# First loads from ScalarE's queue, LoRA lots held behind them, a new order of set one's copies, and inputs laid out by partition

## The chip, the core and the metric

The kernel runs on one core of a Trainium2 chip. The metric is the device time of one execution in microseconds (us), lower is better. The core has a matrix engine (TensorE, PE in the profile, with PEld for its weight loads), VectorE (DVE), ScalarE (ACT), GpSimd (POOL) and SyncE (SP), which here does nothing but issue transfers. Transfers are issued by SP or by ACT. Engines are in order: an instruction that waits holds all that stand behind it on its engine.

## The reference, cut to what matters

```python
# x [2, 1024, 256]; ids [2], the LoRA expert of each sequence; F = 1024, E = 8, TOP_K = 2
h = x @ wi.T + 2 * (x @ common_a.T) @ common_b.T + 2 * (x @ own_a[ids].T) @ own_b[ids].T
h = relu(h)
c = h @ wo.T + (the same two LoRA terms for the way down)
probs = softmax(mean(c, over tokens) @ gate_w)          # one router decision per sequence
top_w, top_i = top_k(probs, 2); top_w /= sum(top_w)
out = x + sum over the two experts e of top_w * (gelu(c @ w1[e] + b1[e]) @ w2[e] + b2[e])
```

All is f32 in and out.

## The kernel before

**Precision.** Every product of two f32 tensors is made of three products of "high" and "low" parts. The high part is a copy to the fp32r type (on ScalarE, functions named `..._high`), the low part is the f32 original less the high part (on VectorE or GpSimd, `..._low`). A product is high x high, high x low and low x high, each a 128 x 128 by 128 x 512 matmul (`three`).

**Work.** Tokens are two sequences (b = 0, 1) of 1,024, each in two halves t of 512. The 1,024 hidden units are cut into four sets of 256. A set q (24 in all: 8 of the conditional part, then 16 of the experts) has an up weight tile `up_raw` and a down weight tile `down_raw` of 256 KB each, a ring of three buffers for each. The hidden layer of a set is four tiles j (two blocks f of hidden units by two token halves t), each in one bank of `hid_ps`; the down products add into the four banks of `out_ps`. Sets 0 to 7 use plain products, sets 8 to 23 a seven-product scheme.

**LoRA.** In the conditional part the LoRA terms are merged into the weights first: TensorE multiplies the two small factors (`raw_up_factor`, `up_factor`, `down_factor`), VectorE adds twice the result to the raw weights (`merge0`, `merge_up`, `merge_down`), and only then come the high and low copies. Set 0 and set 1 take their up factors raw from `lora_first` and `lora_second`; all others need the split factors in `lora_st`, which come from five lots of 192 KB a sequence, (b, 0) to (b, 4), each with a high copy on ScalarE (`lora_high`) and two low halves (`lora_low`). The down weights of set 0 need lot (0, 1), the up weights of set 2 need (0, 0) and (0, 3), the down weights of set 1 need (0, 1) and (0, 2).

**The beginning.** TensorE does twelve warm-up products, the raw factors (L823), then `first_pair(0)` and `first_pair(1)`: set 0's hidden tiles for token half 0 and then half 1, in the order high x high (L743), the low of x (L747), the low of the weights (L751), 12 products each. Then come the down factor of set 0 (L845), tiles 0 and 1 of set 1 (12 products on lines 700, 701 and 704), `down(0, 0)`, the up factor of set 2 (L835), `down(0, 1)`, the down factor of set 1 (L845), and so on in a repeating order. The order on each engine is written out by hand; semaphores tie them together. x arrives in four transfers: half 0 of sequence 0 as two pieces (below called x0[0] and x0[1], by kd, the half of the model dimension, 256 KB each), half 1 of it in one (x0b, 512 KB), and sequence 1 (1 MB). Before the change, ScalarE's queue issues x0[0] and the up weights of set 0; all the rest goes out from SyncE, in the order lora_first, lora_second, x0[1], up weights of set 1, x0b, then the lots and weights in turn. ScalarE's first instructions are these two issues, then its table load, then the copies.

**Waits that matter below.** `hid_high(1, 0)` overwrites the hidden tile that `down(0, 0)` reads, so it waits for it; `lora_high(0, 2)` stands behind it. `bank_free` makes tile j of set q wait for `hid_low(q - 1, j)`. The up factor of set 2 uses bank 3 and waits for `hid_low(0, 3)`.

Of the kernel before, what the change touches and what calls it, by code (L numbers as in the profile page):

```python
# [19 lines left out]
def build(nc, ids, xT, wiT, woT, lora, gate, w1, w2, b12, outT):  # L20
    D, NTOK = xT.shape
    F = wiT.shape[1]
# [90 lines left out]
    LORA_LO_AT = {0: [(0, 3), (0, 2)], 1: [(0, 4)], 2: [(1, 0)], 3: [(1, 1), (1, 2)], 4: [(1, 3), (1, 4)]}  # L113
# [6 lines left out]
    with ExitStack() as ctx:  # L120
# [9 lines left out]
        x_sb = sb("x_sb", [P, KD, NTOK])  # L130
# [66 lines left out]
        s_x0lo = [sem(f"s_x0lo{kd}") for kd in range(KD)]  # L197
# [78 lines left out]
        def raw_tile(p, kd, t):  # L276
            return x_sb[:, kd, half(1, t)] if p == 0 else y_sb[:, kd, t * TOK:(t + 1) * TOK]
# [6 lines left out]
        def store_final(eng, n):  # L284
# [4 lines left out]
                          x_sb[:, kd, at + cols.start:at + cols.stop]).then_inc(s_out, 16)  # L289
# [4 lines left out]
        def _(eng):  # L294
# [37 lines left out]
            eng.dma_start(x_sb[:, :, SEQ:2 * SEQ], xT[:, SEQ:2 * SEQ].rearrange("(k p) t -> p k t", p=P))\  # L332
# [19 lines left out]
            for b in range(NB):  # L352
                for k in range(TOP_K):
# [4 lines left out]
                    for i in range(SETS):  # L358
                        q = N_COND + (TOP_K * b + k) * SETS + i
                        eng.wait_ge(*up_lo_made(q - NU))  # L360
                        src = w1[bass.ds(e_bk, 1), :, i * SW:(i + 1) * SW].rearrange("e (k p) f -> p (e k) f", p=P)
                        eng.dma_start(up_raw[:, q % NU, 0:4 * P].rearrange("p (k f) -> p k f", k=KD), src)\
                           .then_inc(s_up_raw[q % NU], 16)
                        eng.wait_ge(s_down_lo, q - ND + 1)
                        src = w2[bass.ds(e_bk, 1), i * SW:(i + 1) * SW, :].rearrange("e (f p) d -> p (e f) d", p=P)
                        eng.dma_start(down_raw[:, q % ND, :].rearrange("p (f d) -> p f d", d=D), src)\
                           .then_inc(s_down_raw[q % ND], 16)

            for n, (kd, t) in enumerate(ENDS):
# [822 lines left out]
```

## Time and profile before

| what | value |
|---|---|
| median of 3 runs | 274.09 us (273.92 to 274.73) |
| the profiled execution's own time | 273.91 us |
| its span, first to last instruction | 272.1 us |
| TensorE busy | 263.6 us, 97% |
| ScalarE busy | 170.8 us, 63% |
| VectorE busy | 162.2 us, 60% |
| GpSimd busy | 149.1 us, 55% |
| moved by transfers | 19.10 MB, 70 GB/s over the span |

Times inside the execution are us from its first instruction. The profiled execution took 273.91 us in all, 1.8 more than its span, and it is 0.18 under the median.

### The profile page before, as it was taken

The numbers are of one execution on the slowest core, as the hardware profiler recorded it, in microseconds if no ns is written. First come the engines' busy times: TensorE is split into PE (matmuls) and PEld (weight loads), VectorE is DVE, ScalarE is ACT, GpSimd is POOL, SyncE is SP. The second block draws the span as 40 slices with busy tenths as digits, with TensorE's granted clock in tenths as the row PEclk, the third lists the DMA queues.
The fourth block names the chain that finished last, engine by engine and source line by source line (L and its number), as shares of the span: only waits on it lengthen the run. The fifth ranks groups of instructions, "written<-read, shape, count | busy, mean of one in ns | idle before, by whom it ended". The sixth has DMA issues, their size and how long they took to land.

```text
span 272.1 us, 3590 instructions
## 1 busy us (share of the span) xinstructions
PE 263.6 (97%) x1156; PEld 213.0 (78%) x1156; DVE 162.2 (60%) x266; ACT 170.8 (63%) x275; POOL 149.1 (55%) x181
## 2 busy tenths in 40 slices
PE   7798999999999999999999999999999999999995
PEld 3466888888888888888888788888788888888883
DVE  1664354342469754667486786666965667665664
ACT  2554543535446448997986977776766776775650
POOL 0466343726565677799709999566365465431100
PEclk9999999999999999999999999999999999999999
DMA  5996302201003221122010322023022025000004
GB/s 148 259 319 203 110 7 70 78 2 40 1 2 118 77 77 41 39 77 78 28 51 0 79 77 79 8 69 78 5 76 78 4 76 184 9 0 4 0 0 154
DMA packets 17266, 19.10 MB, mean 70 GB/s; under 512 B 2016, under 2 KB 14592, under 8 KB 17248
## 3 DMA queue, kind: packets, MB, share of 16 engines
q1 hardware_dynamic: 16544, 17.96, 21.9%
q10 hardware_dynamic: 704, 0.92, 1.1%
q8 instruction: 9, 0.15, 0.2%
q14 instruction: 9, 0.07, 0.1%
HBM read 16.77 MB, written 2.10 MB: 69 GB/s over the span
## 4 chain that ended last, share of the span: by engine, by line
PE 93%; DMA 2%; DVE 1%; ACT 1%; SPq 1%; issue 1%; POOL 0%; DVEq 0%; POOLq 0%
PE out_ps L700 16%; PE out_ps L701 16%; PE out_ps L704 16%; PE hid_ps L700 14%; PE hid_ps L701 14%; PE hid_ps L704 14%; DMA x_sb<-in_xT 2%; PE hid_ps L845 1%; PE hid_ps L835 1%; SPq L296 1%; PE hid_ps L747 1%; DVE act_lo L261 0%; DVE up_raw L950 0%; ACT up_hi L535 0%; PE hid_ps L751 0%
## 5 line engine op out<-in xcount | busy, mean ns | idle before, releaser
L700 PE MATMUL out_ps<-hid_hi,down_hi 128*128 128x512 f32 x192 | 75.0, 391 | 0.3 <-issue 0.3
L403 POOL TENSOR_TENSOR up_lo<-up_raw,up_hi 128x512 fp32r<-128x512 f32 x39 | 50.4, 1311 | 45.4 <-ACT up_hi L535 45.3
L701 PE MATMUL out_ps<-hid_lo,down_hi 128*128 128x512 f32 x192 | 74.7, 389 | 0.0
L704 PE MATMUL out_ps<-hid_hi,down_lo 128*128 128x512 f32 x192 | 74.7, 389 | 0.0
L700 PE MATMUL hid_ps<-act_hi,up_hi 128*128 128x512 f32 x168 | 65.7, 391 | 0.0
L701 PE MATMUL hid_ps<-act_lo,up_hi 128*128 128x512 f32 x168 | 65.5, 390 | 0.0
L704 PE MATMUL hid_ps<-act_hi,up_lo 128*128 128x512 f32 x168 | 65.4, 389 | 0.0
L567 ACT ACTIVATE hid_ps<-hid_ps,bias_sb 128x512 f32<-128x512 f32 x64 | 42.2, 659 | 29.7 <-DVE hid_ps L990 19.0
L966 DVE SCALAR_TENSOR_TENSOR hid_lo<-hid_ps,mix,hid_hi 128x512 fp32r<-128x512 f32 x64 | 47.8, 747 | 18.7 <-ACT hid_hi L581 18.2
L409 POOL TENSOR_TENSOR down_lo<-down_raw,down_hi 128x512 fp32r<-128x512 f32 x24 | 31.7, 1321 | 44.0 <-ACT down_hi L545 43.9
L581 ACT ACTIVATE hid_hi<-hid_ps,mix 128x512 fp32r<-128x512 f32 x64 | 44.1, 688 | 4.6
L700 PEld LDWEIGHTS out_ps<-hid_hi,down_hi 128*128 128x128 f32 x192 | 36.0, 188 | 8.6 <-issue 1.1
L704 PEld LDWEIGHTS out_ps<-hid_hi,down_lo 128*128 128x128 f32 x192 | 36.0, 188 | 7.6
L701 PEld LDWEIGHTS out_ps<-hid_lo,down_hi 128*128 128x128 f32 x192 | 36.1, 188 | 7.3
L575 ACT ACTIVATE hid_hi<-hid_ps 128x512 fp32r<-128x512 f32 x32 | 18.9, 595 | 30.9 <-PE out_ps L704 29.3
L990 DVE TENSOR_TENSOR hid_ps<-hid_ps,r_sb 128x512 f32<-128x512 f32 x48 | 31.9, 694 | 8.5 <-PE hid_ps L704 8.5
L700 PEld LDWEIGHTS hid_ps<-act_hi,up_hi 128*128 128x128 f32 x168 | 31.6, 188 | 6.7 <-ACT r_sb L552 0.4
L704 PEld LDWEIGHTS hid_ps<-act_hi,up_lo 128*128 128x128 f32 x168 | 31.5, 188 | 6.7
L701 PEld LDWEIGHTS hid_ps<-act_lo,up_hi 128*128 128x128 f32 x168 | 31.6, 188 | 5.9
L966 DVE SCALAR_TENSOR_TENSOR hid_lo<-hid_ps,hid_hi 128x512 fp32r<-128x512 f32 x32 | 21.8, 683 | 22.1 <-ACT hid_hi L575 22.0
L535 ACT ACTIVATE up_hi<-up_raw 128x1024 fp32r<-128x1024 f32 (+1 forms) x23 | 21.3, 925 | 10.0 <-DVE up_raw L950 5.7
L981 DVE TENSOR_TENSOR r_sb<-hid_ps,r_sb 128x512 f32<-128x512 f32 x16 | 11.0, 690 | 16.1 <-PE hid_ps L704 16.0
(91 smaller groups left out, 217.2 us busy)
## 6 DMA issues: line engine op xcount, KB each, us to landing
up_raw<-in_w SPq DMA_DIRECT2D x16, 256.0 KB, 3.0
down_raw<-in_w SPq DMA_DIRECT2D x16, 256.0 KB, 2.7
down_raw<-in_woT SPq DMA_DIRECT2D x8, 256.0 KB, 3.1
lora_raw<-in_lora SPq DMA_DIRECT2D x10, 192.0 KB, 4.6
up_raw<-in_wiT SPq DMA_DIRECT2D x7, 256.0 KB, 3.7
outT<-x_sb SPq DMA_DIRECT2D x6, 256.0 KB, 3.2
x_sb<-in_xT SPq DMA_DIRECT2D x1, 1024.0 KB, 10.5
x_sb<-in_xT SPq DMA_DIRECT2D x1, 512.0 KB, 6.3
```

The lines of the kernel that those rows point to most:

```text
L403: ins = eng.tensor_tensor(up_lo[:, n, cols], up_raw[:, n, cols], f32(up_hi[:, n, cols]), ALU.subtract)
L409: eng.tensor_tensor(down_lo[:, n, :], down_raw[:, n, :], f32(down_hi[:, n, :]), ALU.subtract)\
L535: eng.activation(up_hi[:, n, 0:up_width(q)], up_raw[:, n, 0:up_width(q)], ACT.Copy).then_inc(s_up_hi, 1)
L567: eng.activation(hid_ps[:, j, :], hid_ps[:, j, :], ACT.Gelu, bias=bias_sb[:, b, k, f:f + 1])\
L575: eng.activation(hid_hi[:, j, :], hid_ps[:, j, :], ACT.Relu).then_inc(s_hid_hi, 1)
L581: eng.activation(hid_hi[:, j, :], hid_ps[:, j, :], ACT.Copy, scale=mix[:, b, k:k + 1])\
L700: eng.matmul(out, w_h, a_h, start=start, stop=False, skip_group_check=onto)
L701: eng.matmul(out, w_h, a_l, start=False, stop=False, skip_group_check=onto)
L704: return eng.matmul(out, w_l, a_h, start=False, stop=stop, skip_group_check=onto)
L966: eng.scalar_tensor_tensor(out=hid_lo[:, j, :], in0=hid_ps[:, j, :], scalar=scalar, in1=f32(hid_hi[:, j, :]), op0=op, op1=ALU.subtract).th ...
L981: eng.tensor_tensor(r3_sb[:, :], hid_ps[:, 2, :], r2_sb[:, :], ALU.add).then_inc(s_r3, 1)
L990: eng.tensor_tensor(hid_ps[:, j, :], hid_ps[:, bank, :], addend[:, :], ALU.add).then_inc(s_add, 1)
```

## The change

Five things are done together.

1. ScalarE's queue now issues five transfers before its first copy: x0[0], the up weights of set 0, x0[1], x0b, the up weights of set 1. SyncE issues lora_first and lora_second, and then waits until x0[1] has landed before it issues the lots and all that stands behind them. Lot (0, 0) goes ahead of the down weights of set 0.
2. Low parts of x: GpSimd now makes x0[0]'s, VectorE the other three. x's low parts have a semaphore for each piece.
3. VectorE now makes the low parts of lots (0, 1), (0, 0) and (0, 3), GpSimd only (0, 2) in this stretch; `merge_down(0)` moves ahead of `hid_low(0, 1)`.
4. ScalarE copies x0b ahead of the up weights of set 1, `hid_high(0, 0)` ahead of them too, lot (0, 1) before `hid_high(0, 1)`, and lot (0, 3) right behind the down weights of set 0.
5. The down products wait for the high part of the down weights first, and for the low part only at the third product of a set. All inputs but the LoRA lots and the small tables are laid out on the host so that each partition's part of a transfer is one piece (2 KB of weights or of x0[0], 4 KB of x0b, 8 KB of sequence 1), and `x_sb` has the same layout.

```diff
-    LORA_LO_AT = {0: [(0, 3), (0, 2)], 1: [(0, 4)], 2: [(1, 0)], 3: [(1, 1), (1, 2)], 4: [(1, 3), (1, 4)]}
+    LORA_LO_AT = {0: [(0, 2)], 1: [(0, 4)], 2: [(1, 0)], 3: [(1, 1), (1, 2)], 4: [(1, 3), (1, 4)]}
...
-        x_sb = sb("x_sb", [P, KD, NTOK])
+        x_sb = sb("x_sb", [P, NB, NT, KD, TOK])
...
-        s_x0lo = [sem(f"s_x0lo{kd}") for kd in range(KD)]
+        s_x0lo = [[sem(f"s_x0lo{kd}{t}") for t in range(NT)] for kd in range(KD)]
...
         def load_up(eng, q):
             n, i = q % NU, q % SETS
-            eng.dma_start(up_raw[:, n, 0:4 * P].rearrange("p (k f) -> p k f", k=KD),
-                          wiT[:, i * SW:(i + 1) * SW].rearrange("(k p) f -> p k f", p=P)).then_inc(s_up_raw[n], 16)
+            eng.dma_start(up_raw[:, n, 0:4 * P], wiT[i, :, :]).then_inc(s_up_raw[n], 16)
 
         def load_down(eng, q):
             n, i = q % ND, q % SETS
-            eng.dma_start(down_raw[:, n, :].rearrange("p (f d) -> p f d", d=D),
-                          woT[i * SW:(i + 1) * SW, :].rearrange("(f p) d -> p f d", p=P)).then_inc(s_down_raw[n], 16)
+            eng.dma_start(down_raw[:, n, :], woT[i, :, :]).then_inc(s_down_raw[n], 16)
 
         def load_x0(eng, kd):
-            eng.dma_start(x_sb[:, kd, half(0, 0)], xT[kd * P:(kd + 1) * P, half(0, 0)]).then_inc(s_x0[kd], 16)
+            eng.dma_start(x_sb[:, 0, 0, kd, :], xT[0, :, 0, kd, :]).then_inc(s_x0[kd], 16)
 
         def up_lo_made(q):
             return (s_up0lo, KD) if q == 0 else (s_up_lo, q)
 
         def x0_low(eng, kd, t):
             eng.wait_ge(s_x0hi, t * KD + kd + 1)
-            eng.tensor_tensor(act_lo[:, 0, kd * NT + t, :], x_sb[:, kd, half(0, t)],
-                              f32(act_hi[:, 0, kd * NT + t, :]), ALU.subtract).then_inc(s_x0lo[kd], 1)
+            eng.tensor_tensor(act_lo[:, 0, kd * NT + t, :], x_sb[:, 0, t, kd, :],
+                              f32(act_hi[:, 0, kd * NT + t, :]), ALU.subtract).then_inc(s_x0lo[kd][t], 1)
...
-            load_x0(eng, 1)
-            next_up(1)
-            eng.dma_start(x_sb[:, :, half(0, 1)], xT[:, half(0, 1)].rearrange("(k p) t -> p k t", p=P))\
-               .then_inc(s_x0b, 16)
+
+            eng.wait_ge(s_x0[1], 16)
             load_lora(0, 1, e)
+            load_lora(0, 0, e)
             next_down(0)
-            load_lora(0, 0, e)
             load_lora(0, 3, e)
             next_up(2)
             load_lora(0, 2, e)
             next_down(1)
             load_lora(0, 4, e)
-            eng.dma_start(x_sb[:, :, SEQ:2 * SEQ], xT[:, SEQ:2 * SEQ].rearrange("(k p) t -> p k t", p=P))\
+            eng.dma_start(x_sb[:, 1, :, :, :], xT[1, :, :, :, :])\
                .then_inc(s_x1, 16)
             next_down(2)
             next_up(3)
...
-            x0_low(eng, 1, 0)
+            x0_low(eng, 0, 0)
             up_low(1)
-            x0_low(eng, 1, 1)
-            after((s_x0lo[1], NT))
-            lora_low(0, 1)
             down_low(0)
             after((s_down_lo, 1))
             lora_lows(0)
...
             load_x0(eng, 0)
             load_up(eng, 0)
+            load_x0(eng, 1)
+            eng.dma_start(x_sb[:, 0, 1, :, :], xT[0, :, 1, :, :]).then_inc(s_x0b, 16)
+            load_up(eng, 1)
             x0_high(0)
             x0_high(1)
             up0_high(0)
             up0_high(1)
-            up_high(1)
             x0b_high(0)
             x0b_high(1)
             hid_high(0, 0)
+            up_high(1)
+            lora_high(0, 1)
             hid_high(0, 1)
-            lora_high(0, 1)
             lora_high(0, 0)
             hid_high(0, 2)
             down_high(0)
+            lora_high(0, 3)
             for q in range(1, NSET):
...
-                if q == 1:
-                    lora_high(0, 3)
...
-            def down_pair(q, j, kd):
+            def down_pair(q, j, kd, low_ready=None):
...
-                    eng.wait_ge(s_down_lo, q + 1)
+                    eng.wait_ge(s_down_hi, q + 1)
                 if q in GROUP_FIRST:
                     out_free(q, j)
                 for kd in range(KD):
-                    ins = down_pair(q, j, kd)
+                    ins = down_pair(q, j, kd, (s_down_lo, q + 1) if j + kd == 0 else None)
                 ins.then_inc(s_down, 1)
...
-            x0_low(eng, 0, 0)
             merge0(0)
             merge0(1)
+            x0_low(eng, 1, 0)
             up0_low(0)
             up0_low(1)
+            x0_low(eng, 0, 1)
             merge_up(1, out_ps[:, 2, :])
-            x0_low(eng, 0, 1)
+            x0_low(eng, 1, 1)
+            lora_low(0, 1)
             hid_low(0, 0)
+            merge_down(0, out_ps[:, 3, :])
             hid_low(0, 1)
-            merge_down(0, out_ps[:, 3, :])
+            lora_low(0, 0)
             hid_low(0, 2)
-            lora_low(0, 0)
+            lora_low(0, 3)
             for q in range(1, N_COND):
...
+    def up_sets(w):
+
+        w = w.reshape(w.shape[:-2] + (D // P, P, F // SW, SW))
+        return np.moveaxis(w, -2, -4).swapaxes(-3, -2).reshape(w.shape[:-4] + (F // SW, P, D // P * SW))
+
+    def down_sets(w):
+
+        w = w.reshape(w.shape[:-2] + (F // SW, SW // P, P, D))
+        return w.swapaxes(-3, -2).reshape(w.shape[:-4] + (F // SW, P, SW // P * D))
...
-        "xT": t(x.reshape(NB * S, D)),
-        "wiT": t(a["L0_cond_wi"]),
-        "woT": t(a["L0_cond_wo"]),
+        "xT": x.reshape(NB, S // TOK, TOK, D // P, P).transpose(0, 4, 1, 3, 2),
+        "wiT": up_sets(t(a["L0_cond_wi"])),
+        "woT": down_sets(t(a["L0_cond_wo"])),
         "lora": np.concatenate(lots, axis=2),
         "gate": a["L0_ffn_gate_w"],
-        "w1": a["L0_ffn_w1"],
-        "w2": a["L0_ffn_w2"],
-
+        "w1": up_sets(a["L0_ffn_w1"]),
+        "w2": down_sets(a["L0_ffn_w2"]),
```

## Rows read from the trace of the kernel before

**Rows 1.** busy by stretch: length, each engine (instructions), PE clock, DMA share, GB/s

```profile
0.00:9.08 9.08, 6.33 (x21) 2.89 (x21) 2.08 (x6) 3.00 (x5) 0.91 (x13) 1.00 0.62 169
...
24.77:268.90 244.13, 244.08 (x1084) 201.18 (x1084) 149.47 (x246) 159.49 (x255) 138.46 (x159) 1.00 0.17 52
268.90:272.10 3.20, 0.00 (x0) 0.00 (x0) 0.88 (x2) 0.00 (x0) 0.00 (x0) 1.00 0.46 164
```

**Rows 2.** timeline of PE: start us, us long, line; idle before, releaser

```profile
5.96 1.12 PE L823 MATMUL out_ps<-lora_first 32*128 32x256 f32 x4 [0.43 <-DMA lora_first<-in_lora]
...
9.08 0.70 PE L743 MATMUL hid_ps<-act_hi,up_hi 128*128 128x512 f32 x2 [1.12 <-ACT up_hi L525]
...
12.44 0.73 PE L743 MATMUL hid_ps<-act_hi,up_hi 128*128 128x512 f32 x2 [0.39 <-ACT act_hi L513]
13.82 0.73 PE L747 MATMUL hid_ps<-act_lo,up_hi 128*128 128x512 f32 x2 [0.65 <-DVE act_lo L261]
...
16.59 0.50 PE L845 MATMUL out_ps<-lora_st 96*128 96x256 f32 x2
...
20.18 0.47 PE L700 MATMUL out_ps<-hid_hi,down_hi 128*128 128x512 f32 x1 [0.35 <-issue]
...
21.92 0.47 PE L835 MATMUL hid_ps<-lora_st 96*128 96x256 f32 x2
...
24.77 0.47 PE L845 MATMUL hid_ps<-lora_st 96*128 96x256 f32 x2 [1.01 <-POOL lora_st L232]
```

**Rows 3.** timeline of ACT, up to 31 us

```profile
1.64 1.28 ACT L509 ACT_TABLE_LOAD   x1 [1.64 <-PEq L1182]
...
8.00 0.63 ACT L509 ACTIVATE act_hi<-x_sb 128x512 fp32r<-128x512 f32 x1 [2.70 <-DMA x_sb<-in_xT]
8.53 0.71 ACT L525 ACTIVATE up_hi<-up_raw 128x256 fp32r<-128x256 f32 x2
...
22.34 0.62 ACT L519 ACTIVATE lora_st<-lora_raw 96x512 fp32r<-96x512 f32 x1
```

**Rows 4.** timeline of SP, the issues of three transfers

```profile
3.61 0.42 SPq L254 DMA_DIRECT2D x_sb<-in_xT  x1
...
4.55 0.47 SPq L322 DMA_DIRECT2D x_sb<-in_xT  x1
5.21 0.34 SPq L302 DMA_DIRECT2D lora_raw<-in_lora  x1
```

**Rows 5.** transfers issued to 30 us: KB each, median us to landing

```profile
lora_raw<-in_lora SPq DMA_DIRECT2D x9, 192.0 KB, 6.5
...
x_sb<-in_xT SPq DMA_DIRECT2D x1, 512.0 KB, 6.3
x_sb<-in_xT ACTq DMA_DIRECT2D x1, 256.0 KB, 3.9
up_raw<-in_wiT ACTq DMA_DIRECT2D x1, 256.0 KB, 4.3
x_sb<-in_xT SPq DMA_DIRECT2D x1, 256.0 KB, 4.4
```

**Rows 6.** timeline of DVE, the first merge of up weights

```profile
6.78 0.77 DVE L937 SCALAR_TENSOR_TENSOR up_raw<-out_ps,up_raw 128x256 f32<-128x256 f32 x2 [0.76 <-PE out_ps L823]
```

**Rows 7.** line 261, low parts of x: ns shortest, median, longest

```profile
L261 DVE TENSOR_TENSOR act_lo<-x_sb,act_hi x2: 691/1020/1348, 5.3 to 12.4; 128x512 fp32r<-128x512 f32 x2
L261 POOL TENSOR_TENSOR act_lo<-x_sb,act_hi x2: 1281/1512/1742, 8.7 to 13.2; 128x512 fp32r<-128x512 f32 x2
```

**Rows 8.** line 232, low parts of lots, up to 30 us

```profile
L232 DVE TENSOR_TENSOR lora_st<-lora_raw,lora_st x2: 415/904/1394, 18.5 to 19.0; 32x256 fp32r<-32x256 f32 x2
```

**Rows 9.** timeline of POOL, low parts of lot (0, 2)

```profile
23.10 1.53 POOL L232 TENSOR_TENSOR lora_st<-lora_raw,lora_st 32x256 fp32r<-32x256 f32 x2 [1.33 <-ACT lora_st L519]
```

**Rows 10.** transfers from 4 to 5 us by queue (q10 ACT's, q1 SP's)

```profile
q1 hardware_dynamic: 104, 0.13, 46.8%
q10 hardware_dynamic: 114, 0.10, 33.4%
```

More of the change, by code:

```diff
@@ L20, in build @@
 def build(nc, ids, xT, wiT, woT, lora, gate, w1, w2, b12, outT):
-    D, NTOK = xT.shape
-    F = wiT.shape[1]
+    D, NTOK = outT.shape
+    F = wiT.shape[0] * 2 * P
     E = w1.shape[0]
@@ L276, in raw_tile @@
         def raw_tile(p, kd, t):
-            return x_sb[:, kd, half(1, t)] if p == 0 else y_sb[:, kd, t * TOK:(t + 1) * TOK]
+            return x_sb[:, 1, t, kd, :] if p == 0 else y_sb[:, kd, t * TOK:(t + 1) * TOK]
         ENDS = [(0, 0), (1, 0), (0, 1), (1, 1)]
@@ L288, in store_final @@
             eng.dma_start(outT[kd * P:(kd + 1) * P, at + cols.start:at + cols.stop],
-                          x_sb[:, kd, at + cols.start:at + cols.stop]).then_inc(s_out, 16)
+                          x_sb[:, NB - 1, t, kd, cols]).then_inc(s_out, 16)
         program = ctx.enter_context(nc.Block())
@@ L360, in _ @@
                         eng.wait_ge(*up_lo_made(q - NU))
-                        src = w1[bass.ds(e_bk, 1), :, i * SW:(i + 1) * SW].rearrange("e (k p) f -> p (e k) f", p=P)
-                        eng.dma_start(up_raw[:, q % NU, 0:4 * P].rearrange("p (k f) -> p k f", k=KD), src)\
-                           .then_inc(s_up_raw[q % NU], 16)
+                        src = w1[bass.ds(e_bk, 1), i, :, :].rearrange("e p c -> (e p) c")
+                        eng.dma_start(up_raw[:, q % NU, 0:4 * P], src).then_inc(s_up_raw[q % NU], 16)
                         eng.wait_ge(s_down_lo, q - ND + 1)
-                        src = w2[bass.ds(e_bk, 1), i * SW:(i + 1) * SW, :].rearrange("e (f p) d -> p (e f) d", p=P)
-                        eng.dma_start(down_raw[:, q % ND, :].rearrange("p (f d) -> p f d", d=D), src)\
-                           .then_inc(s_down_raw[q % ND], 16)
+                        src = w2[bass.ds(e_bk, 1), i, :, :].rearrange("e p c -> (e p) c")
+                        eng.dma_start(down_raw[:, q % ND, :], src).then_inc(s_down_raw[q % ND], 16)
             for n, (kd, t) in enumerate(ENDS):
                 eng.wait_ge(s_fin, n + 1)
-                eng.dma_start(outT[kd * P:(kd + 1) * P, half(0, t)], x_sb[:, kd, half(0, t)]).then_inc(s_out, 16)
+                eng.dma_start(outT[kd * P:(kd + 1) * P, half(0, t)], x_sb[:, 0, t, kd, :]).then_inc(s_out, 16)
             for n in (0, 2, 4):
@@ L508, in x0_high @@
                 eng.wait_ge(s_x0[kd], 16)
-                eng.activation(act_hi[:, 0, kd * NT, :], x_sb[:, kd, half(0, 0)], ACT.Copy).then_inc(s_x0hi, 1)
+                eng.activation(act_hi[:, 0, kd * NT, :], x_sb[:, 0, 0, kd, :], ACT.Copy).then_inc(s_x0hi, 1)
             def x0b_high(kd):
                 eng.wait_ge(s_x0b, 16)
-                eng.activation(act_hi[:, 0, kd * NT + 1, :], x_sb[:, kd, half(0, 1)], ACT.Copy).then_inc(s_x0hi, 1)
+                eng.activation(act_hi[:, 0, kd * NT + 1, :], x_sb[:, 0, 1, kd, :], ACT.Copy).then_inc(s_x0hi, 1)
             def lora_high(b, lot):
@@ L598, in raw_high @@
                     eng.wait_ge(s_x1, 16)
-                    src = x_sb[:, kd, SEQ:2 * SEQ]
+                    src = x_sb[:, 1, :, kd, :]
                 else:
@@ L775, in down_pair @@
                              (hid_hi[:, j, :], hid_lo[:, j, :]), q in GROUP_FIRST and j == mine[0],
-                             q in GROUP_LAST and j == mine[1])
+                             q in GROUP_LAST and j == mine[1], low_ready)
             def out_free(q, j):
@@ L996, in result @@
                 for kd in range(KD):
-                    eng.scalar_tensor_tensor(out=x_sb[:, kd, half(b, t)], in0=out_ps[:, kd * NT + t, :],
-                                             scalar=mixed_b2[:, b, 1, kd:kd + 1], in1=x_sb[:, kd, half(b, t)],
+                    eng.scalar_tensor_tensor(out=x_sb[:, b, t, kd, :], in0=out_ps[:, kd * NT + t, :],
+                                             scalar=mixed_b2[:, b, 1, kd:kd + 1], in1=x_sb[:, b, t, kd, :],
                                              op0=ALU.add, op1=ALU.add).then_inc(s_fin, 1)
@@ L1135, in _ @@
             for n, (kd, t, cols) in enumerate(FINAL):
-                at = half(NB - 1, t).start
-                mine = slice(at + cols.start, at + cols.stop)
+                x = x_sb[:, NB - 1, t, kd, cols]
                 eng.wait_ge(s_done, ENDS.index((kd, t)) + 1)
-                eng.scalar_tensor_tensor(out=x_sb[:, kd, mine], in0=out_ps[:, kd * NT + t, cols],
-                                         scalar=mixed_b2[:, NB - 1, 1, kd:kd + 1], in1=x_sb[:, kd, mine],
+                eng.scalar_tensor_tensor(out=x, in0=out_ps[:, kd * NT + t, cols],
+                                         scalar=mixed_b2[:, NB - 1, 1, kd:kd + 1], in1=x,
                                          op0=ALU.add, op1=ALU.add).then_inc(s_final, 1)
```

7 lines of the change are left out of this document (3 added, 4 removed).

## The prediction, made before the change was run

> **What bounds the kernel now.** I read the busy time by stretch first, then what TensorE waited for, then the timelines of the first 31 us. The table has its answer in one row: from 24.77 to 268.90 us TensorE is busy for 244.08 of 244.13 us [rows 1], 1,084 products at 0.225 us apiece, at the full granted clock of 1.00 (its 2.4 GHz level). After 24.77 nothing that arrives earlier can help, and the tail behind the last product (3.20 us) holds the same instructions in both kernels. So whatever the change is worth, it is worth by moving the down factor of set 1, which starts at 24.77 [rows 2], and every other engine's work behind it hangs on semaphores that move with it.
>
> From its first real product at 9.08 to 24.77 TensorE has 48 products of 512 columns (10.8 us at 0.225) and two factor steps of 0.34 and 0.31, 11.45 in all [rows 2]. 24.77 less 9.08 is 15.69, so 4.24 us are waits: pair 0 to pair 1 takes 3.36 for 2.7 of work (the 12.44 row, x0b late); 12.44 to 13.82 takes 1.38 for two products, 0.45 (VectorE's low part of x), and the rest of pair 1, to 16.59, holds another 0.5; the start of `down(0, 0)` at 20.18 comes 3.59 after the down factor at 16.59, for 0.34 and 2.7 of work; the up factor at 21.92 comes 1.74 after it for 1.35; and 24.77 comes 2.85 after that, for 0.31 and 1.35 [rows 2]. That is 0.66, 0.93, 0.5, 0.55, 0.4 and 1.2. Ahead of 9.08 TensorE waits on ScalarE: x0[1] lands at 8.0 (3.61 and 4.4), is copied from 8.00, and only then come the copies of set 0's merged up weights at 8.53 [rows 3, 4, 5].
>
> **The change part by part.** Landings are a transfer's issue plus its time to landing [rows 4, 5]: now x0[1] 8.0, x0b 10.85, lot (0, 1) 11.7 (with the median of nine).
>
> *Start.* x0[1] is issued third by ScalarE, at 1.65 instead of 3.61 (issues cost 0.42 to 0.47 [rows 4]). If all the 1.96 us counted it would land at 6.0; if the engines and not the issue are what it waits for, still at 8.0. I take 6.6, nearer the early end, because lora_first no longer stands ahead of it in its queue. Its copy ends at 7.2. Now the merge is as late: raw factors need lora_first, first product 5.96, merge from 6.78, two halves in 0.77, so the first is done at 7.2 and the second at 7.55 [rows 2, 6]. The copy of the first half of set 0 takes 0.40 (two in 0.71 [rows 3]), and TensorE follows 0.15 after it, as 8.53 and 0.40 led to 9.08. So the first product goes from 9.08 to 7.75: **1.33 less**. With x0[1] later than 6.6 the start moves one for one. Three more issues on ScalarE (1.3 us) push its table load from 1.64 to 2.95 and its end to 4.25; x0[0] lands at 4.64 (0.74 and 3.9 [rows 5]), so this is hidden by 0.4 us.
>
> *Low parts of x.* GpSimd makes x0[0]'s (1.28 us [rows 7]) at 5.4 to 6.7, needed at 8.2. VectorE makes x0[1]'s from 7.5 to 8.2 (0.69 uncontended [rows 7]), needed at 9.1, then set 0's low weights until 9.0, needed at 9.55. VectorE and GpSimd block each other when both read only SBUF: 0.69 became 1.35, and for a half lot 0.415 became 1.39 [rows 7, 8]. Here they no longer meet in this stretch. Pair 0 is then 2.7 without a wait: 7.75 to 10.45.
>
> *x0b and set 1's up weights.* x0b is issued at 2.1 instead of 4.55 and no longer behind the 256 KB of up weights. Ends: 8.4 (2.45 earlier) and 10.85. I take 8.7. Its copies end at 9.35 and 9.9, needed at 10.45 and 11.35. Up weights of set 1 now stand behind it: I take 9.5 (from 8.6, 4.08 and the 4.5 or so of the others, to 10.85). VectorE then does x0b's first low part 9.4 to 10.1, `merge_up(1)` to 10.7, the second low part to 11.35, needed at 11.8. Pair 1 has no wait either: 10.45 to 13.15.
>
> *The wait on SyncE.* Behind it stand all lots, the down weights of sets 0 to 2, up weights of sets 2 and 3, and x of sequence 1. The first issue there moves from 5.21 to 6.65, but with 1 MB less ahead in its queue. Ends for lot (0, 1): 9.55, with three quarters of the 3.9 that 256 KB took on an empty queue, and 13.1, with the 6.5 of now [rows 5]. I take 10.5, nearer the empty queue that it finds, and 0.8 more for each next one. ScalarE wants (0, 1) at 11.35, (0, 0) at 12.4, (0, 3) at 15.3; VectorE the down weights at 14.1. Hidden by 0.9 us and more; past that it costs one for one. Sets 2 on are wanted at 19 and later.
>
> *Lots on VectorE.* ScalarE copies lot (0, 1) at 11.35 to 11.95. VectorE's two halves then meet GpSimd's low part of set 1's up weights (11.5 to 12.8); blocked as in [rows 8] they end at 13.45 instead of 12.8. The down factor of set 0 starts at 13.45 against 16.59: 0.3 of wait is new. `hid_low(0, 0)` stands behind them and ends at 14.1, and set 1's first tile waits for it; 0.3 again. Its 12 products end at 16.85. `merge_down(0)` from 14.1 to 14.8, `down_high(0)` to 15.45, GpSimd's low part to 16.9. `down(0, 0)` now starts on the high part at 16.85 and wants the low part at 17.3: the 0.55 of wait is gone. **20.18 becomes 16.85, 3.33 less.**
>
> *What is late next.* Two things feed 24.77. From `down(0, 0)`: its end frees the tile, ScalarE copies it and then lot (0, 2) (22.34), GpSimd makes the low parts in 1.53 from 23.10, TensorE follows [rows 2, 3, 9]. None of this is changed, so the distance 20.18 to 24.77, 4.59, stays: 16.85 and 4.59 is 21.45. The other: VectorE has `lora_low(0, 0)` against GpSimd's 1.3 us (ends 17.3, blocked again), `hid_low(0, 2)` to 17.95, `lora_low(0, 3)` to 18.75, `hid_low(0, 3)` to 19.4, and the up factor of set 2 waits for that; 19.4, 0.31 and 1.35 is 21.1. It is hidden by 0.35. So 24.77 becomes 21.45.
>
> *Layout.* Half as many rows for each weight transfer. With 1 KB rows 256 KB took 4.3 from ScalarE's queue and with 2 KB rows 3.9 [rows 5], so a load gains between 0 and 0.4; I take 0, since the loads up to 21 us are hidden above and those behind it feed a TensorE that never waits [rows 1]. The copy of sequence 1 from two pieces instead of one: nothing, for the same reason.
>
> **Sum.** 1.33 (start), 0.66, 0.93, 0.5 and 0.55 (waits that go), less 0.6 (two new ones): 3.4, and by the rounded steps above 3.3, which 24.77 moves by, since what lies between `down(0, 0)` and it keeps its length. Against its own time: 273.91 less 3.3 is 270.6. The median is 0.18 above that execution, so 270.7.
>
> **A page against the estimate.** The Trainium skill, page "DMA: Bandwidth & Descriptors", section "Issuing engines are not separate DMA queues", says that a second issuing engine saves only the sequencer's issue time. By that rule x0[1] can gain at most the 1.96 us, which the sum respects, and bytes that had landed by a certain time land no sooner; this is the late-loads rival below, at the time that is worked out there from rows.
>
> **Rivals.** *x0[1] as late as before* (it is the read and not the issue). The start stays at 9.08, the later waits still go: 3.3 less 1.3, 271.9. For it: x0[0], alone in its queue, took 3.9 too [rows 5].
>
> *Late loads.* x0b and set 1's up weights need, with all that is ahead, the same 1,632 KB that had landed at 10.85. If the up weights land then, `merge_up(1)` ends at 12.0, the low part of x0b behind it at 12.65 (0.35 of wait), ScalarE's copy, GpSimd's low part and the blocked lot slip by 1.2, and the down factor starts at 14.65: 3.3 less 1.2, 271.9. The lot at its late end, 13.1, gives the same: copied to 13.7, its low parts to 14.6 (GpSimd is done by then). Against it: from 4 to 5 us the engines were 0.80 busy (46.8% and 33.4% [rows 10]), so there is room.
>
> *The queues are drained in the order of issue, as one* (the slower side). Then lora_first, issued at 2.64, stands behind all five of ScalarE's transfers, and the start is its landing plus 1.8. It decides from a landing of 9.2 us on (now 5.9, and 3.3 of gain); with the 1,632 KB landed at 10.85 the start is at 12.65 and the sum 4.9 less 3.3 on the wrong side: 275.5. Against it: from 4 to 5 us packets of both queues were served side by side [rows 10], though ScalarE's were issued 1.5 us ahead.
>
> *The gain is given back*: the first 25 us shrink, and a wait opens behind 24.77, for instance on a load held back on SyncE. 273.9. For it only that such waits do not show until something moves; against it that the only clocks there are semaphores of TensorE's own progress.
>
> **Chances.** Forecast 0.66, x0[1] late 0.12, late loads 0.12, drained as one 0.04, given back 0.06. The likeliest has 270.1 to 271.3 of its own (landings of x0[1] 0.5 either way, one more or one fewer blocking). The range reaches to the two at 271.9 and half a us beyond, and down to 269.9, where lora_first too lands 0.7 sooner: 269.9 to 272.4. A measurement here can tell 0.3%, 0.8 us, from no change; faster by more holds the first three, 0.90; the same 0.06; slower 0.04.
>
> **What would show it.** x0[1]'s copy starting near 6.6 and TensorE's first L743 near 7.75; no wait at the second L743 and the second L747; L845 of set 0 near 13.45, released by VectorE; `down(0, 0)` near 16.85; L845 of set 1 near 21.45, released by GpSimd's lot (0, 2); from there on 244.1 us of uninterrupted products. Wrong if lora_first lands later than 6.5, if the low part behind `merge_up(1)` ends after 11.8, if `hid_low(0, 3)` ends after 19.7, or if the stretch behind set 1's down factor is longer than 244.13.

## The result: 0.4% slower, where 1.2% faster was forecast

| | before | changed |
|---|---|---|
| median, 22 executions each | 274.1 us (273.56 to 274.92) | 275.63 us (274.42 to 276.68) |
| ratio, with its 95% interval | | 1.0044 (1.0029 to 1.0059) |
| the profiled execution | 273.91 us, span 272.1 | 274.78 us, span 273.0 |

The forecast was 270.7 with a range up to 272.4. The direction was wrong.

The busy time by stretch of the changed kernel: up to pair 0, pair 0 itself, and from the down factor of set 1 on. The columns are those of [rows 1]: length, busy time of PE, PEld, DVE, ACT and POOL, granted clock, DMA share, GB/s.

```profile
0.00:10.00 10.00, 7.46 (x21) 2.97 (x21) 2.10 (x6) 3.68 (x6) 1.80 (x13) 1.00 0.75 235
10.00:14.44 4.44, 4.44 (x14) 3.50 (x14) 2.25 (x5) 0.94 (x3) 0.00 (x0) 0.62 1.08 280
...
25.59:269.70 244.11, 244.02 (x1084) 201.18 (x1084) 149.56 (x247) 160.11 (x256) 138.57 (x159) 1.00 0.16 52
269.70:273.00 3.30, 0.00 (x0) 0.00 (x0) 0.85 (x2) 0.00 (x0) 0.00 (x0) 1.00 0.46 161
```

The last two rows are as forecast: 244.11 us in which TensorE is busy for 244.02, against 244.13 and 244.08 in [rows 1], and a tail of 3.3 against 3.2. Nothing was gained or lost behind the down factor of set 1. That factor starts at 25.59 instead of 24.77 [rows 2] or the forecast 21.45; the whole result is in front of it. The second row has one of the two reasons: a mean granted clock of 0.62 in pair 0, where the same stretch of the kernel before has 1.00:

```profile
9.08:12.44 3.36, 2.97 (x13) 2.14 (x13) 2.14 (x4) 1.36 (x4) 1.40 (x2) 1.00 1.03 281
```

The other is the length of the first row. The timeline of TensorE in the changed kernel, with the columns of [rows 2] (the first row is the warm-up products):

```profile
1.20 5.30 PE L872 MATMUL hid_ps<-y_sb 128*128 128x512 bf16 x12 [1.20 <-DVE y_sb L1059]
7.59 1.13 PE L817 MATMUL out_ps<-lora_first 32*128 32x256 f32 x4 [1.09 <-DMA lora_first<-in_lora]
8.97 1.10 PE L817 MATMUL out_ps<-lora_second,lora_first 32*128 32x256 f32 x4 [0.25 <-DMA lora_second<-in_lora]
10.00 0.78 PE L737 MATMUL hid_ps<-act_hi,up_hi 128*128 128x512 f32 x2
...
14.44 0.62 PE L737 MATMUL hid_ps<-act_hi,up_hi 128*128 128x512 f32 x2
...
17.44 0.50 PE L839 MATMUL out_ps<-lora_st 96*128 96x256 f32 x2
18.25 0.47 PE L694 MATMUL hid_ps<-act_hi,up_hi 128*128 128x512 f32 x1 [0.31 <-DVE hid_lo L960]
...
21.07 0.39 PE L694 MATMUL out_ps<-hid_hi,down_hi 128*128 128x512 f32 x1
...
23.60 0.50 PE L829 MATMUL hid_ps<-lora_st 96*128 96x256 f32 x2 [1.01 <-DVE hid_lo L960]
...
25.59 0.48 PE L839 MATMUL hid_ps<-lora_st 96*128 96x256 f32 x2
```

The raw factors wait 1.09 us for lora_first, the second four for lora_second, and the first real product starts at 10.00, not at 7.75 as forecast or 9.08 as before. Then pair 0 takes 4.44 us for 2.7 us of work. From 14.44 on each piece has the length that was forecast within a quarter of a us: 3.00, 3.63 and 4.52 us where the prediction had 3.0, 3.4 and 4.6, with the forecast waits on VectorE in front of 18.25 (0.31) and 23.60 (1.01). Where lora_first was is in the view of transfers issued up to 30 us (columns of [rows 5]):

```profile
x_sb<-in_xT ACTq DMA_DIRECT2D x2, 256.0 KB, 3.8
...
x_sb<-in_xT ACTq DMA_DIRECT2D x1, 512.0 KB, 5.2
lora_first<-in_lora SPq DMA_DIRECT2D x1, 64.0 KB, 4.9
lora_second<-in_lora SPq DMA_DIRECT2D x1, 32.0 KB, 5.6
```

The up weights of set 1 alone, ScalarE's last load, in the same view cut to the time of their issue:

```profile
up_raw<-in_wiT ACTq DMA_DIRECT2D x1, 256.0 KB, 6.0
```

And ScalarE's timeline, with the last two of its five issues:

```profile
2.12 0.45 ACTq L626 DMA_DIRECT2D x_sb<-in_xT  x1
2.60 0.45 ACTq L247 DMA_DIRECT2D up_raw<-in_wiT  x1
3.09 1.28 ACT L502 ACT_TABLE_LOAD   x1 [3.09 <-issue]
4.42 0.63 ACT L502 ACTIVATE act_hi<-x_sb 128x512 fp32r<-128x512 f32 x1
5.69 0.63 ACT L502 ACTIVATE act_hi<-x_sb 128x512 fp32r<-128x512 f32 x1 [0.64 <-DMA x_sb<-in_xT]
```

SyncE issued lora_first at 2.63, 0.03 us behind ScalarE's last load, and it landed 4.9 us later, at 7.55; in the kernel before it had been issued at the same time and its first product ran at 5.96 [rows 2]. Between 4 and 5.5 us, well after both issues, only ScalarE's queue moves anything:

```profile
DMA packets 259, 0.59 MB, mean 391 GB/s; under 512 B 30, under 2 KB 30, under 8 KB 259
...
q10 hardware_dynamic: 259, 0.59, 104.3%
```

In the kernel before, both queues moved packets from 4 to 5 us [rows 10]. From 6 to 7.5 us both queues move packets in the changed kernel too:

```profile
q10 hardware_dynamic: 179, 0.35, 68.8%
q1 hardware_dynamic: 105, 0.13, 34.8%
```

So lora_first landed behind the first four of ScalarE's loads (the fourth, x0b, at 7.3), but not behind the fifth: the up weights of set 1, issued 0.03 us ahead of it, landed at 8.6, 1.1 us after it.

What arrived early did so by more than forecast: x0[0] was copied at 4.42 and x0[1] at 5.69, where 6.6 was taken for the latter and 6.0 had been the early end, and x0b landed at 7.3 (2.12 and 5.2), where 8.7 was taken. It bought nothing, since the copy of set 0's up weights needs the merge and the merge needs lora_first.

### The profile page after: what moved, and what is told of

Same layout as the page of the kernel before. It is cut to its first block, busy times and chain, and to the rows that moved or that the text cites. A ratio compares the mean times of both kernels' runs of the same rounds, so it can differ in the third digit from the quotient of the medians.

```text
span 273.0 us, 3575 instructions
## 1 busy us (share of the span) xinstructions
PE 265.6 (97%) x1156; PEld 214.6 (79%) x1156; DVE 163.5 (60%) x271; ACT 171.1 (63%) x275; POOL 144.6 (53%) x176
## 4 chain that ended last, share of the span: by engine, by line
PE 92%; DVE 3%; DMA 2%; SPq 1%; ACT 1%; issue 0%; DVEq 0%
PE out_ps L694 16%; PE out_ps L698 16%; PE out_ps L695 16%; PE hid_ps L694 14%; PE hid_ps L695 14%; PE hid_ps L698 14%; DMA lora_second<-in_lora 2%; DVE lora_st L234 2%; DVE hid_lo L960 1%; PE hid_ps L839 1%; PE hid_ps L829 1%; PE hid_ps L741 1%; SPq L296 1%; PE hid_ps L737 1%; PE out_ps L817 0%
```

## The experiments

The three parts of the change are called the layout, the queues (ScalarE's five loads and SyncE's wait) and the order (of copies and low parts). All ratios are to the kernel before on the same chip. A "fall" is a stretch at the low clock. One like that in the second row above takes the mean clock of the execution from 1.00 to 0.993 or 0.994 (the changed kernel's profile has 0.994); 0.987 or 0.988 is about twice that time at the low clock. The diffs are against the changed kernel unless another is named.

**e1: lora_first ahead of x0b and set 1's up weights.**

```diff
 # ScalarE
             load_x0(eng, 1)
-            eng.dma_start(x_sb[:, 0, 1, :, :], xT[0, :, 1, :, :]).then_inc(s_x0b, 16)
-            load_up(eng, 1)
 # SyncE, behind lora_second
+            eng.dma_start(x_sb[:, 0, 1, :, :], xT[0, :, 1, :, :]).then_inc(s_x0b, 16)
+            next_up(1)
             eng.wait_ge(s_x0[1], 16)
```

> The changed kernel, with x0b and set 1's up weights issued by SyncE behind lora_second instead of by ScalarE ahead of it; ScalarE keeps x0[0], the up weights of set 0 and x0[1]. Theory A (transfers are served in the order of issue whatever the queue, so lora_first landed at 7.55 behind 1,280 KB): lora_first lands near 6.0, behind 768 KB, the raw factors start there instead of at 7.59, the first L737 near 7.9 instead of 10.00, and if the granted clock then stays at 1.00 the time is 2.5 to 4 us under the changed kernel's 274.6, near 271. Theory B (the loss is VectorE's new order in set one): lora_first may land earlier, but the down factor of set 1 stays near 25.5 and the time within 0.8 us of the changed kernel's. Theory C (lora_first is late because SyncE's own queue starts late): lora_first still lands after 7 us.

Measured: 271.85 us, ratio 0.9915 (0.9903 to 0.9928). (In the changed kernel 1,536 KB are issued ahead of lora_first; the 1,280 KB of the expectation are what landed ahead of it.) The landing of lora_first and TensorE's timeline:

```profile
lora_first<-in_lora SPq DMA_DIRECT2D x1, 64.0 KB, 3.6
```

```profile
6.29 1.12 PE L816 MATMUL out_ps<-lora_first 32*128 32x256 f32 x4 [0.50 <-DMA lora_first<-in_lora]
...
8.33 1.22 PE L736 MATMUL hid_ps<-act_hi,up_hi 128*128 128x512 f32 x2
...
12.79 0.62 PE L736 MATMUL hid_ps<-act_hi,up_hi 128*128 128x512 f32 x2
...
23.93 0.47 PE L838 MATMUL hid_ps<-lora_st 96*128 96x256 f32 x2
```

Issued at 2.64, lora_first lands at 6.25, and the first product starts 1.67 us earlier than in the changed kernel. Of theory A the early landing and the time hold, though the start is at 8.33 and not near 7.9; B and C fall: the order on VectorE is the same and 23.93 is 1.66 ahead of 25.59. This profiled execution still has the slow clock in pair 0 (8.33 to 12.79 is 4.46 us), and it is the longest of the six: 273.13 at a mean clock of 0.993, the other five 271.16 to 271.95 at 0.998 to 1.000. So one fall of the clock costs some 1.3 us here. Of the 3.5 us by which e1 is under the changed kernel by the ratios, the earlier start is worth some 1.5 (273.13 against the changed kernel's 274.58, the median of its executions with one fall); the rest is that the clock falls in one of six executions and not in all. In all runs the loads in front of lora_first were ScalarE's; whether large loads of SyncE's own queue would hold up a small one of ScalarE's was not tried.

**e2: four more warm-up products.** The edit is `WARM_UP = 16`.

> The changed kernel with 16 warm-up products instead of 12, nothing else. They fill the gap from 6.50 to 7.59 in which TensorE has nothing to do. Theory A with the clock as a second loss (pair 0 ran at a granted clock of 0.50 from 10.53 to 13.95 because TensorE had idled before it): the clock stays at 1.00, pair 0 takes 2.7 instead of 4.4 us, and the time is 1.3 to 1.7 us under the changed kernel's. Theory D (the clock is a lottery of the execution and the gap has no part in it): no difference to the changed kernel within 0.5 us, and the clock still falls in the profiled execution.

Measured: 273.11 us, ratio 0.9981 (0.9963 to 0.9999), so some 1.7 to 2.5 under the changed kernel by the medians. TensorE's timeline:

```profile
1.20 5.39 PE L872 MATMUL hid_ps<-y_sb 128*128 128x512 bf16 x16 [1.20 <-DVE y_sb L1059]
7.49 1.13 PE L817 MATMUL out_ps<-lora_first 32*128 32x256 f32 x4 [0.91 <-DMA lora_first<-in_lora]
...
9.94 0.73 PE L737 MATMUL hid_ps<-act_hi,up_hi 128*128 128x512 f32 x2
...
12.79 0.62 PE L737 MATMUL hid_ps<-act_hi,up_hi 128*128 128x512 f32 x2
...
23.96 0.47 PE L839 MATMUL hid_ps<-lora_st 96*128 96x256 f32 x2
```

lora_first is as late as ever (7.49), the start is at 9.94, but pair 0 is over at 12.79, 2.85 us. Nine of the twelve executions have a mean clock of 0.998 or more and take 272.87 to 273.28; the three at 0.993 and 0.994 take 274.30 to 275.21. The changed kernel has no execution over 0.994 among 33 (22, and 11 more in e12): 17 have one fall, 0.993 or 0.994, and a median of 274.58; 16 have 0.981 to 0.988, twice as long at the low clock or longer, and a median of 276.18. Theory D falls: four more products make the falls rare. That they do it by filling the gap is not shown. In this profile the sixteen products took 5.39 us, hardly longer than the twelve of the changed kernel (5.30), 0.91 us of gap were left in front of lora_first against 1.09, and the clock did not fall.

**e3: the layout alone.** The kernel before with loads and `x_sb` by partition; all issues, copies and low parts in the old order.

> The kernel before with the new layout alone (inputs by partition, x_sb too): loads issued from the old queues in the old order, old order of copies and low parts. Theory A: landings come 0.5 to 1.5 us earlier in the first 20 us, because packets of 2 KB and more are served faster; the start moves with x0[1] alone, so 0 to 1.5 us under the kernel before. Rival: no difference (0.3 us), since TensorE waits for other engines and not for bytes.

Measured: 274.04 us, ratio 1.0000 (0.9990 to 1.0011). The rival holds. x0[1] still came for a start at 9.16:

```profile
9.16 1.19 PE L739 MATMUL hid_ps<-act_hi,up_hi 128*128 128x512 f32 x2 [1.21 <-ACT up_hi L522]
...
13.41 0.61 PE L739 MATMUL hid_ps<-act_hi,up_hi 128*128 128x512 f32 x2
...
16.69 0.50 PE L841 MATMUL out_ps<-lora_st 96*128 96x256 f32 x2
...
24.88 0.47 PE L841 MATMUL hid_ps<-lora_st 96*128 96x256 f32 x2 [0.98 <-POOL lora_st L234]
```

This profile says one thing more. The clock fell here too, pair 0 takes 4.25 us (9.16 to 13.41) instead of 3.36, and yet the down factor of set 0 is at 16.69 and that of set 1 at 24.88, 0.1 behind [rows 2]. The kernel before waits for x0b behind pair 0 anyway, and the slow products fit into that wait. It shows in the times of the kernel before that were taken beside e1 to e12: 24 at a clock of 0.998 to 1.000 have a median of 273.95, 32 at 0.992 to 0.994 one of 274.00; only the six with 0.987 or 0.988 are longer, 274.79. One fall of the clock is free in the old kernel and costs 1.3 us (e1) to 1.9 (e9) in one that no longer waits.

**e4: layout and new order, old queues.**

> The changed kernel with its loads issued as before the change (x0[1], set 1's up weights and x0b by SyncE behind lora_second, no wait on SyncE, old order of down weights and lot (0, 0)); new layout and new order of copies and low parts stay. Theory A: lora_first lands near 5.9, the start is as in the layout alone, and the new order saves the waits in pair 1 and before down(0, 0): 2 to 3 us under the kernel before. Theory B (the new order is what costs): slower than the layout alone by 0.8 us or more.

Measured: 273.84 us, ratio 0.9981 (0.9964 to 0.9999). Neither: 2 to 3 us were expected and 0.2 to 0.5 came. With the old queues x0[1] lands as late as before; the start is at 9.53. Only two of twelve executions were free of a fall, and these took 272.39 and 272.44, 1.6 under before; in the other ten the waits of the old order are replaced by a slow pair 0 (4.33 us in the profile). The new order saves 1.6 us where the clock stays up (e3's three executions without a fall have a median of 274.05) and 0.2 where it falls. This is a miss of A in the median, and what A left out was the clock.

**e5: layout and queues, old order.**

> The changed kernel with the old order of copies and low parts; the new layout, ScalarE's five loads and SyncE's wait stay. Theory A (order of issue): lora_first lands near 7.5 as in the changed kernel, so the first product of set 0 starts near 10.0; x0b is there early but the old order copies it only behind set 1's up weights, so waits in pair 1 stay: 0.5 to 1.5 us over the kernel before, 274.6 to 275.5. Theory B (the new order of low parts is what costs): under the kernel before, since x0b and set 1's weights land 2 us earlier.

Measured: 275.82 us, ratio 1.0079 (1.0049 to 1.0110). The raw factors start at 7.87, the first product at 10.20. The time is 0.3 over theory A's range. The queues alone do the damage, and the new order does not add to it; theory B falls.

**e6: e1 with 16 warm-up products.** `WARM_UP = 16` on e1.

> e1 (x0b and set 1's up weights issued by SyncE behind lora_second) with 16 warm-up products. The two losses should be separate: the earlier lora_first gave 2.8 us at the median, and the clock still fell in e1's profiled execution (273.13 against its median of 271.85). Theory A with the clock: the time is e1's best, 271.2 to 271.8, the high single times of e1 go, the clock stays at 1.00 in the profile. Rival: warm-up products do nothing once lora_first is early; median 271.85 and one in six executions near 273 as in e1.

Measured: 272.10 us, ratio 0.9935 (0.9922 to 0.9948). The expectation is missed: no clock under 0.998 in five executions, but the median is not better than e1's. e7's profile suggests why.

**e7: the two chains behind `down(0, 0)`.** On e6:

```diff
-    LORA_LO_AT = {0: [(0, 2)],
+    LORA_LO_AT = {0: [(0, 3), (0, 2)],
 # ScalarE, set 1
+                if q == 1:
+                    lora_high(0, 2)
                 if cond(q):
                     hid_high(q, 0)
-                    if q == 1:
-                        lora_high(0, 2)
 # VectorE, set 0
             hid_low(0, 2)
-            lora_low(0, 3)
```

> e6 with two edits to what feeds set 2's up factor and set 1's down factor: GpSimd makes lot (0, 3)'s low parts again (VectorE's hid_low(0, 3) moves up by 0.86), and ScalarE copies lot (0, 2) ahead of hid_high(1, 0), not behind it. Theory (both chains named in the prediction bind, each by about 1 us): the wait before L828 of 1.0 and the one before L838 of 0.3 go down by 0.9 in all, and the time is 0.7 to 1.2 us under e6. Rival: GpSimd's queue (low parts of the down weights, then two lots) becomes the late one, and the time is e6's within 0.3 us.

Measured: 271.43 us, ratio 0.9896 (0.9883 to 0.9910), 1.1 us under e6 by the ratios. The wait of 1.01 before the up factor of set 2 is 0.15, and the down factor of set 1 comes 1.71 behind it, not 1.98. Three rows of this profile bear on e6:

```profile
1.20 6.57 PE L871 MATMUL hid_ps<-y_sb 128*128 128x512 bf16 x16 [1.20 <-DVE y_sb L1058]
7.69 1.13 PE L816 MATMUL out_ps<-lora_first 32*128 32x256 f32 x4
...
9.61 0.72 PE L736 MATMUL hid_ps<-act_hi,up_hi 128*128 128x512 f32 x2
```

lora_first had landed at 6.35, but the sixteen warm-up products took 6.57 us here, until 7.77 (5.16 in e6's profile, which is e6's fastest execution), so the raw factors started at 7.69 and the first product at 9.61. Warm-up products that outlast the load they cover delay what stands behind them. That the slower executions of e6 are such ones is likely and not shown.

**e8: only x0b behind lora_second.** Set 1's up weights stay on ScalarE's queue.

> The changed kernel with only x0b moved behind lora_second on SyncE's queue; set 1's up weights stay on ScalarE's. A dose between e1 and the changed kernel: bytes issued ahead of lora_first are 1,024 KB, against 768 KB in e1 (landed 6.25) and 1,536 KB less the last, issued in the same 0.03 us, in the changed kernel (landed 7.55). Theory A (order of issue): lora_first lands at 6.6 to 7.0 and the first L737 starts between e1's 8.33 and the changed kernel's 10.00, near 8.8 to 9.1. Rival (only x0b with its 4 KB packets holds lora_first up): it lands at 6.25 as in e1.

Measured: 275.77 us, ratio 1.0049 (1.0032 to 1.0067). The landing:

```profile
lora_first<-in_lora SPq DMA_DIRECT2D x1, 64.0 KB, 5.0
```

That is 7.65, later than expected (6.6 to 7.0) and no better than in the changed kernel, with a third less ahead of it; the size of the dose was missed. What holds is the order: the up weights of set 1, issued 0.5 us ahead of it, land at 7.2, then lora_first, lora_second and x0b follow in the order of their issue. The rival, that only x0b is in the way, falls. What is left open is why 512 KB less ahead of it brought lora_first no earlier (7.65 against 7.55): the bytes ahead do not give the landing.

**e9: e7 with 12 warm-up products.**

> e7 with 12 warm-up products instead of 16 (so: the changed kernel, x0b and set 1's up weights on SyncE behind lora_second, lot (0, 3)'s low parts on GpSimd, lot (0, 2) copied ahead of hid_high(1, 0)). In e7's profile the 16 products ran at the low clock until 7.77 and held the raw factors back from 6.35 to 7.69. Theory: 12 products lose nothing on that side, so the median is 0 to 0.5 us under e7's ratio of 0.9896, and 0.7 to 1.2 us under e1. Rival: without the four products the clock falls more often and the median is over e7's.

Measured: **270.36 us, ratio 0.9879 (0.9855 to 0.9902)**, the best version. TensorE's timeline:

```profile
1.19 5.29 PE L871 MATMUL hid_ps<-y_sb 128*128 128x512 bf16 x12 [1.19 <-DVE y_sb L1058]
6.42 1.13 PE L816 MATMUL out_ps<-lora_first 32*128 32x256 f32 x4
...
8.34 0.73 PE L736 MATMUL hid_ps<-act_hi,up_hi 128*128 128x512 f32 x2
...
19.55 0.47 PE L828 MATMUL hid_ps<-lora_st 96*128 96x256 f32 x2 [0.19 <-POOL lora_st L234]
...
21.25 0.40 PE L838 MATMUL hid_ps<-lora_st 96*128 96x256 f32 x2
```

Five of six executions have a clock of 1.000 and take 269.91 to 270.63; the sixth has a fall and takes 272.15. By the ratios e9 is 1.0 us under e1, as expected, and 0.5 under e7, where the two intervals overlap. The down factor of set 1 is at 21.25, which is where the prediction had put it (21.45), by another way: 0.6 later at the start, and 0.8 less behind it. The 0.6 at the start is the warm-up again: lora_first landed at 5.9, and the twelve products ran until 6.48.

**e10: e1's queues, old order.**

> e1's queues (three loads on ScalarE, x0b and set 1's up weights behind lora_second on SyncE, wait on SyncE) with the old order of copies and low parts. It fills the table of load order by copy order. Theory: the new order pays only where the data is early, so here it should show: e10 is 1.5 to 2.5 us over e1 (ratio near 0.998 to 1.000 of before). Rival: the queues alone make e1's gain and the order is worth nothing, e10 within 0.4 us of e1.

Measured: 273.92 us, ratio 0.9993 (0.9976 to 1.0011), 2.1 us over e1. The theory holds. What TensorE waited for, us in total, times, longest:

```profile
PE hid_ps L740 <- ACT act_hi L510: 1.4, 1, 1.4
...
PE hid_ps L744 <- DVE act_lo L261: 0.7, 1, 0.7
```

The start is at 7.99, 1.1 earlier than before, but x0b is copied behind set 1's up weights, and the two waits in pair 1 (1.4 and 0.7) eat all of it. The table of medians is then:

| loads issued | old order | new order |
|---|---|---|
| as before | 274.04 (e3) | 273.84 (e4) |
| five from ScalarE, as in the change | 275.82 (e5) | 275.63 (the change) |
| three from ScalarE, lora_first fourth | 273.92 (e10) | 271.85 (e1) |

In the first two lines the clock fell in most executions (9 and 10 of 12 in e3 and e4, all in e5 and the changed kernel), in the third in 2 of 12 and 1 of 6. So the lateness of the data is not the only thing that differs between the lines: where the clock stayed up, the order was worth 1.6 us with the old queues too (e4).

**e11: e1 without SyncE's wait.** `eng.wait_ge(s_x0[1], 16)` is taken out.

> e1 without SyncE's wait for x0[1]: the lots are issued from about 4.9 on instead of 6.05. Theory A (transfers are served in the order of issue): x0b and set 1's up weights are issued ahead of the lots and land when they did (8.5 and 9.4), so the time is e1's within 0.4 us: holding back buys nothing. Rival (transfers in flight share the engines): x0b and the up weights land 0.5 us or more later and the time rises by as much.

Measured: 271.68 us, ratio 0.9920 (0.9900 to 0.9940), the same as e1's 0.9915. In this profile x0b and the up weights landed at 9.3 and 10.6, 0.8 and 1.1 later than in e1's, which is the rival's landing, but the time did not follow; and with the wait in place e9's and e10's profiles have them as late (9.1 and 10.4, 9.4 and 10.4). Holding the lots back buys nothing in time.

**e12: the changed kernel again, beside e9 to e11.**

> The changed kernel itself, on the same chip as e9 to e11, so that they are compared with it side by side. Expected: the ratio to before of its 22 executions, 1.0044 (1.0029 to 1.0059); lora_first again after 7.3; times in two groups near 274.6 and 276.2, by whether the granted clock falls once or twice in the first 20 us.

Measured: 274.81 us, ratio 1.0049 (1.0027 to 1.0070), in the two groups that were expected (seven executions up to 274.85, three from 275.95 to 276.5), and one execution at 277.23 with a clock of 0.981.

## Why the prediction was wrong

**The bound was right.** All that counts lies ahead of the down factor of set 1; the stretch behind it kept its 244.1 us and the rival that looked there ("given back") did not happen.

**The step that failed is the start.** "Now the merge is as late: raw factors need lora_first, first product 5.96" took lora_first's landing from the old trace, although the change put three more loads, 1,024 KB, ahead of it in the order of issue. The prediction had this as a rival, "the queues are drained in the order of issue, as one", gave it 0.04, and argued against it with [rows 10], packets of both queues between 4 and 5 us. The rows were read for too much: at that time ScalarE's queue had only the rest of 512 KB left, so both could be in service without lora_first having overtaken anything. The prediction's own sign of being wrong, a landing of lora_first later than 6.5, came true: 7.55. The rival was right in the main and not to the letter, since the last of ScalarE's loads landed behind lora_first, and its size was wrong: its 10.85 for the landing was that of the same bytes in the old trace, and from 4 to 5.5 us the loads now ran at 391 GB/s, where [rows 10] have 0.23 MB in 1 us. That its 275.5 is near the measured 275.63 is luck: its start was 12.65, the real one 10.00, and the clock, which it did not have, made up the rest. By the prediction's own formula a landing at 7.5 would have cost 1.6 and left a gain of 1.7. lora_second, which TensorE takes in order behind it, was forgotten there; it landed at 8.8 and made the start 10.00, 2.25 late.

**The second step that failed is silent in the text**: twelve products "2.7 without a wait", at a clock of 1.00 taken from [rows 1]. TensorE idled from 6.50 to 7.59 and for 0.25 before 8.97, with the raw factors' narrow products (32 rows) between and behind; about three us after the first gap (0.77 over 10 to 11 us) the granted clock fell to 0.50, its 1.2 GHz level, and pair 0 took 4.44, 1.74 more. The stretch from 11 to 13 us has it, in the columns of [rows 1]:

```profile
11.00:13.00 2.00, 2.00 (x6) 1.61 (x5) 1.25 (x3) 0.00 (x0) 0.00 (x0) 0.50 1.06 275
```

e2 shows that four more warm-up products make it rare (273.11 in the median), and e3 that the old kernel has such falls too but hides one behind x0b. The change took the cover away in the same move that brought the fall into all of its 33 executions. Why the clock falls stays open: the idle time alone does not tell, since the profiled execution of the kernel before waited 0.43 and 1.12 us ahead of pair 0 [rows 2] without a fall, and e1's only 0.50 with one.

**The sum then closes.** 270.6 and 2.25 and 1.74 is 274.6; the rest, 0.2, is in set 1's tiles (3.63 for 3.4). The profiled execution took 274.78. The median of the 22, 275.63, is among the twelve executions with a clock of 0.987 or 0.988 (275.58 to 276.68), which spend twice as long at the low clock; e8's profile (0.988) is such a one, with 0.50 in every us from 9 to 15. In parts: e2's executions without a fall, near 273.0, carry the late lora_first alone, 2.3 over the forecast.

**The page.** The Trainium skill, page "DMA: Bandwidth & Descriptors", section "Issuing engines are not separate DMA queues", says that the loads of all issuing engines run on the same DMA engines and interleave. The changed kernel's trace agrees for 6 to 7.5 us, where both queues moved packets (0.35 and 0.13 MB); from 4 to 5.5 us, 1.4 us and more after lora_first's issue, it shows packets of ScalarE's queue alone.

**What held.** x0[1], x0b and the weights land earlier, by more than taken. The waits in pair 1 and before `down(0, 0)` are gone (e1 against e10: 2.1 us). VectorE's lots are blocked by GpSimd as forecast: the two halves of a lot take 1.54 and 1.85 against 0.86 when GpSimd is idle, and `hid_low(0, 3)` at 22.86 is what the up factor of set 2 waits for:

```profile
15.84 1.54 DVE L234 TENSOR_TENSOR lora_st<-lora_raw,lora_st 32x256 fp32r<-32x256 f32 x2 [3.59 <-ACT lora_st L512]
...
19.36 1.85 DVE L234 TENSOR_TENSOR lora_st<-lora_raw,lora_st 32x256 fp32r<-32x256 f32 x2
...
21.96 0.86 DVE L234 TENSOR_TENSOR lora_st<-lora_raw,lora_st 32x256 fp32r<-32x256 f32 x2
22.86 0.69 DVE L960 SCALAR_TENSOR_TENSOR hid_lo<-hid_ps,hid_hi 128x512 fp32r<-128x512 f32 x1
```

That this path and the lot (0, 2) path were both near binding was right, and e7's two edits together took 1.1 us from them. The layout costed at nothing was right (e3). The table load's cover held, barely: it ends at 4.37, and the copy of x0[0] starts at 4.42.

## What to carry to other kernels

When loads are moved to another queue, list every load by its time of issue over all queues and take that as the first guess of the order of landing; the small one that opens the critical chain has to be issued before the large ones, and a wait that holds others back can't help one that is already behind. Where a change removes waits, look at what the waits were hiding, and try each part against each: here the order of copies was worth 0.2 us where a slow first pair of tiles covered the waits anyway, and 2.1 us where the data came early and the clock stayed up. Fill TensorE's gaps at the start only up to the landing that ends them.

## What the runs showed of the hardware

Transfers of two queues landed in the order of issue in the profiles of e1 and e8. In the changed kernel they did so but for one: lora_first, issued 0.03 us behind the up weights of set 1, landed at 7.55 and these at 8.6, and it is the same in e2, e5 and e12 (7.4 to 7.8 against 8.5 to 9.2). In e5 and e12 even lora_second, issued 0.6 us behind the up weights, landed ahead of them (8.75 against 9.2, 8.6 against 8.9). So the order of issue gave the landings in the main, and small loads passed the last large one. Whether this is decided where they are issued or on the DMA engines, and whether ScalarE's queue has a part in it as such, was not tried.

TensorE's clock fell in some executions of every kernel that was timed here except e6 and e7. By the time at which lora_first landed in the profile and the number of warm-up products, with the new layout and x0[1] from ScalarE's queue:

| lora_first | warm-up products | executions with a fall |
|---|---|---|
| 7.4 to 7.8 us (the changed kernel, e5, e8) | 12 | 43 of 43 |
| 7.5 us (e2) | 16 | 3 of 12 |
| 5.9 to 6.3 us (e1, e9, e10, e11) | 12 | 5 of 30 |
| 6.0 to 6.4 us (e6, e7) | 16 | 0 of 10 |

Both the earlier load and the four products made falls rare. What exactly brings a fall about was not settled.
